# A layer of gated delta attention: the convolution taps of each head go round their three chains inside VectorE's places for that head

## The reference

```
outs = [dwconv_causal(x, w) for w in (ms_w3, ms_w15, ms_w31)]
y = jnp.concatenate(outs, axis=1)
y = y.reshape(b, h, 3 * d, l).transpose(0, 3, 1, 2)
y = y @ kernel_mix_w
```

## Time and profile before

| | us |
|---|---|
| median of 3 runs | 3498.72 |
| lowest and highest of them | 3491.64, 3504.08 |
| the profiled execution | 3488.17 |
| its span, from the first to the last instruction | 3485.9 |
| TensorE matmul busy (share of the span) | 3314.3 (95%) |
| VectorE busy | 3162.7 (91%) |
| ScalarE busy | 2760.5 (79%) |
| GpSimd busy | 824.9 (24%) |
| VectorE's taps (L1924), 5408 instructions | 2256.8 |

### The profile page before, as it was taken

The page is one execution under the profiler, slowest core; times in us unless marked ns, Lnnn a source line. Parts: engine busy times, 40 slices in busy tenths (PEclk is TensorE's granted clock), DMA queues, the critical chain, the costliest instruction groups (busy, mean ns, idle before and its releaser), DMA issues.

```text
span 3485.9 us, 70437 instructions
## 1 busy us (share of the span) xinstructions
PE 3314.3 (95%) x22880; PEld 2429.7 (70%) x22880; DVE 3162.7 (91%) x7841; ACT 2760.5 (79%) x9146; POOL 824.9 (24%) x1501
## 2 busy tenths in 40 slices
PE   7999999999999999999999999999999999999988
PEld 6666777667776677776777766777766777766764
DVE  6998999999898999999998999999999999999994
ACT  5777888778887778887788877788877788777874
POOL 2322221122221222211222212222112222112220
PEclk9999999999999999999999999999999999999999
DMA  6022211122211222111222112221112221112211
GB/s 188 18 40 51 51 33 39 31 51 51 49 30 26 50 51 51 37 37 29 51 51 50 29 31 45 51 51 40 34 29 51 51 51 32 39 32 51 45 30 21
DMA packets 188310, 154.96 MB, mean 44 GB/s; under 512 B 111804, under 2 KB 146108, under 8 KB 187688
## 3 DMA queue, kind: packets, MB, share of 16 engines
q0 software_dynamic: 31744, 79.70, 13.2%
q1 hardware_dynamic: 156200, 70.76, 7.7%
HBM read 51.34 MB, written 52.95 MB: 30 GB/s over the span
## 4 chain that ended last, share of the span: by engine, by line
DVE 30%; PE 27%; ACT 20%; issue 10%; DMA 9%; POOL 3%; SPq 0%; ACTq 0%; DVEq 0%; POOLq 0%
DVE my L1924 24%; PE dense L811 7%; DMA my<-prod 5%; PE dense L744 3%; PE dense L734 3%; ACT my L1361 3%; PE small L757 2%; ACT dense L1394 2%; PE cell L703 2%; PE dense L721 2%; DMA rows_out<-Bm 2%; PE cell L704 2%; POOL Tu L461 1%; POOL Xu L464 1%; DMA Bu<-rows_out 1%
## 5 line engine op out<-in xcount | busy, mean ns | idle before, releaser
L1924 DVE SCALAR_TENSOR_TENSOR my<-vT,mw,my 128x256 f32<-128x256 f32 x5408 | 2256.8, 483 | 44.8 <-DMA my<-prod 26.1
L422 POOL TENSOR_SCALAR vare<-xsq 128x2 f32<-128x2 f32 x32 | 6.0, 187 | 2008.3 <-ACT xsh L1104 2008.3
L811 PE MATMUL dense<-xsh,w 128*128 128x256 f32 x2016 | 474.5, 381 | 3.8
L811 PEld LDWEIGHTS dense<-xsh,w 128*128 128x128 f32 x2016 | 362.6, 190 | 70.9 <-ACT xr L1426 10.9
L1334 ACT ACTIVATE ka<-dense 128x512 f32<-128x512 f32 x64 | 38.2, 596 | 304.2 <-PE dense L721 304.2
L721 PE MATMUL dense<-xk,wfk 128*128 128x256 f32 x1024 | 239.7, 388 | 11.9 <-DVE xb L1992 11.7
L734 PE MATMUL dense<-wr,xr 128*128 128x512 f32 x512 | 241.2, 605 | 0.0
L744 PE MATMUL dense<-wfv,ka 128*128 128x512 f32 x512 | 238.2, 598 | 0.0
L574 PE MATMUL front<-xsh,wq 128*128 128x256 f32 x1024 | 236.5, 384 | 0.3 <-ACT raw L1142 0.3
L574 PE MATMUL front<-xsh,wv 128*128 128x256 f32 x1024 | 232.9, 386 | 2.7 <-ACT xsh L1119 2.7
L721 PEld LDWEIGHTS dense<-xk,wfk 128*128 128x128 f32 x1024 | 192.0, 192 | 62.0 <-issue 37.0
(11 more groups left out here) (188 smaller groups left out, 6806.3 us busy)
## 6 DMA issues: line engine op xcount, KB each, us to landing
my<-prod POOLq DMA_DIRECT2D x160, 384.0 KB, 4.2
xa<-in_x SPq DMA_DIRECT2D x32, 512.0 KB, 4.4
rows_out<-Bm SPq DMA_DIRECT2D x64, 256.0 KB, 4.2
out<-xb POOLq DMA_DIRECT2D x32, 512.0 KB, 14.7
Yq<-units_out SPq DMA_DIRECT2D x128, 32.0 KB, 2.3
w<-in_w SPq DMA_DIRECT2D x1, 2048.0 KB, 17.2
Bu<-rows_out SPq DMA_DIRECT2D x32, 64.0 KB, 3.0
units_out<-Xu SPq DMA_DIRECT2D x32, 64.0 KB, 2.5
```

What stands on the lines that cost most here:

```text
L811: e.matmul(by_batch(o), w1[:, k, hs(2 * pair + c)], xsh[s % 2][:, k, :, 1:1 + P], start=(k == 0), stop=False)
L1924: i = e.scalar_tensor_tensor(o, vT[s % 2][:, c, :, off:off + P], mw[:, col:col + 1], o, ALU.mult, ALU.add)
```

## The change

Only the order of calls in `vector_program` changes, and within it only the order of the taps of each head among the places which the taps of that head have. All other calls keep their place, counted in instructions, and no engine gets another instruction. In the loop, the new order goes round the three chains of a head. In head 2, where block 2 has 29 taps for VectorE and the others 13, block 2 has every second place and the other two share the rest. In the prologue and the epilogue, calls with adjoining ranges are written as one; the order there is the old one.

The head of the loop (head 3), the end of the loop's head 1 and the start of its head 2; what is left out follows the same patterns:

```
             for i in range(2, NS):
                 step_Y(i - 2)
-                taps(i - 2, 3, 9, 10)
+                taps(i - 2, 3, 5, 6)
                 taps(i - 2, 2, 34, 35)
                 taps(i - 2, 2, 53, 54)
-                taps(i - 2, 3, 5, 6)
-                taps(i - 2, 3, 8, 9)
+                taps(i - 2, 3, 8, 10)
                 turn_Y(i - 2, 1)
                 taps(i - 2, 3, 11, 12)
+                taps(i - 2, 3, 13, 14)
                 taps(i - 2, 3, 12, 13)
                 taps(i - 2, 3, 14, 15)
-                taps(i - 2, 3, 13, 14)
+                taps(i - 2, 3, 16, 17)
+                taps(i - 2, 3, 15, 16)
                 taps(i - 2, 3, 17, 18)
...
                 taps(i - 2, 3, 53, 54)
+                taps(i - 2, 3, 55, 56)
                 taps(i - 2, 3, 54, 55)
-                taps(i - 2, 3, 49, 50)
-                taps(i - 2, 3, 52, 53)
+                gate_value(i - 2, 0)
                 taps(i - 2, 3, 56, 57)
-                gate_value(i - 2, 0)
+                taps(i - 2, 3, 58, 59)
...
                 add_state(i - 2, 1)
-                taps(i - 1, 1, 13, 14)
-                taps(i - 1, 1, 15, 16)
-                taps(i - 1, 1, 10, 11)
-                taps(i - 1, 1, 17, 18)
+                taps(i - 1, 1, 11, 15)
                 norms_add(i - 1)
                 norms_inv(i - 1)
...
                 gains(i - 1)
-                taps(i - 1, 1, 20, 21)
-                taps(i - 1, 1, 22, 23)
-                taps(i - 1, 1, 25, 26)
-                taps(i - 1, 1, 24, 25)
-                taps(i - 1, 1, 27, 28)
+                taps(i - 1, 1, 23, 26)
+                taps(i - 1, 1, 0, 1)
+                taps(i - 1, 1, 26, 27)
                 softmax_sum(i - 2)
...
                 make_aT(i - 1, 0)
                 make_aT(i - 1, 1)
+                taps(i - 1, 2, 2, 3)
+                taps(i - 1, 2, 0, 1)
+                taps(i - 1, 2, 5, 6)
+                taps(i - 1, 2, 3, 4)
+                taps(i - 1, 2, 8, 9)
                 taps(i - 1, 2, 1, 2)
-                taps(i - 1, 2, 0, 1)
+                taps(i - 1, 2, 11, 12)
+                taps(i - 1, 2, 6, 7)
+                taps(i - 1, 2, 14, 15)
                 taps(i - 1, 2, 4, 5)
-                taps(i - 1, 2, 3, 4)
+                taps(i - 1, 2, 17, 18)
+                taps(i - 1, 2, 9, 10)
+                taps(i - 1, 2, 20, 21)
                 taps(i - 1, 2, 7, 8)
-                taps(i - 1, 2, 2, 3)
-                taps(i - 1, 2, 10, 11)
-                taps(i - 1, 2, 5, 6)
-                taps(i - 1, 2, 8, 9)
-                taps(i - 1, 2, 6, 7)
-                taps(i - 1, 2, 9, 10)
-                taps(i - 1, 2, 11, 12)
-                taps(i - 1, 2, 14, 15)
-                taps(i - 1, 2, 17, 18)
+                taps(i - 1, 2, 23, 24)
                 taps(i - 1, 2, 12, 13)
```

More of the change, by code:

```diff
@@ L2007, in vector_program @@
             taps(0, 0, 2, 3)
[L2008 to L2014, removed]
+            taps(0, 1, 1, 3)
+            taps(0, 1, 4, 7)
+            taps(0, 0, 3, 5)
             taps(0, 1, 7, 8)
@@ L2049, in vector_program @@
             gains(0)
-            taps(0, 1, 23, 24)
-            taps(0, 1, 24, 25)
-            taps(0, 1, 25, 26)
+            taps(0, 1, 23, 26)
             taps(0, 1, 3, 4)
@@ L2055, in vector_program @@
             taps(0, 1, 26, 27)
-            taps(0, 1, 28, 29)
-            taps(0, 1, 29, 30)
+            taps(0, 1, 28, 30)
             taps(0, 2, 5, 6)
@@ L2111, in vector_program @@
             taps(0, 2, 36, 37)
-            taps(0, 2, 49, 50)
-            taps(0, 2, 50, 51)
+            taps(0, 2, 49, 51)
             taps(0, 2, 28, 29)
@@ L2120, in vector_program @@
             taps(0, 3, 1, 2)
-            taps(0, 3, 3, 4)
-            taps(0, 3, 4, 5)
+            taps(0, 3, 3, 5)
             taps(0, 3, 7, 8)
@@ L2153, in vector_program @@
                 taps(i - 2, 3, 35, 36)
-                taps(i - 2, 3, 24, 25)
+                taps(i - 2, 3, 37, 38)
+                taps(i - 2, 3, 36, 37)
                 taps(i - 2, 3, 38, 39)
-                taps(i - 2, 3, 27, 28)
-                taps(i - 2, 3, 25, 26)
+                taps(i - 2, 3, 40, 41)
+                subtract_state(i - 2, 1)
+                taps(i - 2, 3, 39, 40)
                 taps(i - 2, 3, 41, 42)
-                taps(i - 2, 3, 30, 31)
-                taps(i - 2, 3, 28, 29)
@@ L2161, in vector_program @@
-                taps(i - 2, 3, 33, 34)
+                taps(i - 2, 2, 54, 55)
+                taps(i - 2, 3, 43, 44)
+                taps(i - 2, 3, 42, 43)
                 taps(i - 2, 3, 44, 45)
-                taps(i - 2, 3, 36, 37)
-                taps(i - 2, 3, 31, 32)
+                subtract_state(i - 2, 0)
+                taps(i - 2, 3, 46, 47)
+                taps(i - 2, 3, 45, 46)
                 taps(i - 2, 3, 47, 48)
-                subtract_state(i - 2, 1)
+                taps(i - 2, 3, 49, 50)
@@ L2167, in vector_program @@
+                taps(i - 2, 3, 48, 49)
                 taps(i - 2, 3, 50, 51)
[L2168 to L2178, removed]
+                taps(i - 2, 3, 52, 53)
@@ L2420, in vector_program @@
             taps(NS - 2, 3, 59, 60)
-            taps(NS - 2, 3, 61, 62)
-            taps(NS - 2, 3, 62, 63)
+            taps(NS - 2, 3, 61, 63)
             taps(NS - 2, 3, 64, 65)
@@ L2497, in vector_program @@
             taps(NS - 1, 1, 3, 4)
-            taps(NS - 1, 1, 28, 29)
-            taps(NS - 1, 1, 29, 30)
+            taps(NS - 1, 1, 28, 30)
             add_two(NS - 2, 0)
@@ L2553, in vector_program @@
             taps(NS - 1, 2, 28, 29)
-            taps(NS - 1, 2, 44, 45)
-            taps(NS - 1, 2, 45, 46)
+            taps(NS - 1, 2, 44, 46)
             make_aT(NS - 1, 0)
@@ L2565, in vector_program @@
             taps(NS - 1, 3, 3, 4)
-            taps(NS - 1, 3, 5, 6)
-            taps(NS - 1, 3, 6, 7)
+            taps(NS - 1, 3, 5, 7)
             taps(NS - 1, 2, 33, 34)
```

208 lines of the change are left out of this document (84 added, 124 removed).

## The result

The changed kernel takes 3586.07 us in the median (3574.16 to 3593.45, 4 runs), the kernel before 3497.98 beside it: 1.0249 of it as the ratio of the runs, 95% interval 1.0214 to 1.0283. By that ratio it is 87 us slower, far outside the range of 3470 to 3507. The profiled execution took 3589.27 us with a span of 3587.0, 101.1 longer than the span before.

What follows compares the result with a forecast made beforehand. No engine had room by itself (TensorE 95%, VectorE 91% busy), so waits decided, with head 3's fourth add limiting the long stretch. Gains of 3.9 + 3 + 2 = 9 us gave 3489.7 us from 3498.7; range 3470 to 3507.

Steps and rivals of the forecast that it cites:

- Price of a seam: VectorE's taps: one directly behind its own chain's tap costs 0.13 us; 12 an iteration, 47 us less VectorE work.
- Part 1: Head 3's seam between step_Y and subtract_state(0): VectorE is last there, so all counts, 3.9 us; bounds 0 and 3.9.
- Part 2: Seams ahead of feature_rest, norms_add and head 2's first tap: hidden by VectorE's waits there, together nothing.
- Part 3: Eight seams from head 2 to head 3's first tap: limited by head 3's fourth add, 0.1 us an iteration, 3 us.
- Part 4: GpSimd's inversion, advancing one instruction per VectorE instruction: fourth add 0.07 us sooner, 2 us, bounds +8 and -12.
- the lock between VectorE and GpSimd: VectorE instructions with two SBUF inputs and GpSimd ones reading SBUF exclude each other; said to change no figure.
- The slower rival: GpSimd's add into out, issued before the fourth add lands, delays it: 12 us loss, 3510.7; chance 0.1.

Runs made afterwards that it cites:

- e15: Kernel before with head 3's taps alone in their new order; 3482.69 us against 3492.59 beside it, ratio 0.9978.
- e17: Kernel before with head 1's taps alone in their new order, heads 2 and 3 old; ratio 1.0007 to the kernel before.
- e9: Changed kernel with one seam only, in head 2, about 4.5 us behind the landing of head 2's add; ratio 1.0035 to the kernel before.
- e11: Changed kernel with TensorE's turn_o(0) moved behind the two calls of project(4), filling its idle time; ratio 1.0274 to the kernel before.
- e10: Changed kernel with one seam only, in head 2, about 1.3 us behind the landing of head 2's add; ratio 1.0263 to the kernel before.
- e5: Changed kernel with one seam only, in head 2, about 3.3 us behind the landing of head 2's add; ratio 1.0046 to the kernel before.
- e7: Changed kernel with one small VectorE instruction, waiting for nothing, added behind head 2's sixteenth tap; ratio 1.0137 to the kernel before.
- e13: Kernel before with ScalarE's products for head 3's fourth add made ahead of copy_oT(1); ratio 1.0063 to the kernel before.

## Why the prediction was wrong

- **Price of a seam: right.** 17 taps shrank from 7.33 to 6.82 us. VectorE's busy time fell by 31.9 us and not 47, because a seam's 0.13 us is part overlap lost (0.08) and part a gap, and the gap never counted as busy.
- **Part 1 (head 3's seam, 3.9 us): right**, and hidden by the rest. The wait ahead of `solve` is 12.9 us where 17.3 - 3.9 = 13.4 was predicted. Alone (e15) the order gains 4.5 to 10.5 us.
- **Part 2 (three seams, nothing): right.** The covering waits grew from 70.1 to 72.3 and from 29.8 to 33.5 us, and e17 is level.
- **Part 3 (3 us, limited by the fourth add): the limit was right, the gain is not seen.** VectorE's wait for adds is 29.9 us in the changed kernel instead of the 50 expected, because VectorE is late as well there: ahead of `add_attention` it waits 76.0 us for `attend`, in the kernel before 9.4. Where GpSimd is on time (e9) the waits become 59 in number and 38.6 us, TensorE's wait for `xb` falls from 11.7 to 0.6 us and its wait for `mask_W`'s result rises from 19.7 to 27.6, as the part described, but no time is won.
- **Part 4 (GpSimd, "I take 0.07 us sooner at the fourth add: 2 us, bounds +8 and -12"): this step failed**, in sign and far beyond its bound. The fourth add lands 2.75 us later, 31 x 2.75 = 85 us. The rule behind it, "advances one instruction per instruction of VectorE", holds where GpSimd got in behind a break: the earlier trace rows show that stretch alone. I carried it over to the first instruction and priced a missed slot at 0.4 us, one tap. In a stream of taps without a break the slot doesn't come back until an instruction of another kind: L456 was released between 4.5 and 6.2 us and ended at 7.67, and L461 behind it lost its turn once more.
- The sentence that the lock between VectorE and GpSimd "changes none of the figures above" was the same mistake. The trace of before had the sign: L456 took 425 ns in the mean and 0.29 us where it had no wait, and its ends lay behind seams. I asked what the seams cost VectorE and not whom they let in.
- **The slower rival** had the right chain (a late fourth add) and the wrong cause. In e9 the add into `out` is issued ahead of the fourth add's landing in 17 of 29 iterations (4 in the kernel before), as the rival said, and the fourth add lands no later: at 28.80 us instead of 28.87.

## What to carry to other kernels

A pause on one engine can be another engine's only way in. Before a bubble is squeezed out, look at which instructions of other engines end just behind it, and ask where they would go instead. An engine that is 24% busy can hold the path: here GpSimd runs nearly without a pause from the inversion to the last add, and 2.31 us at its start cost 87 us in the changed kernel, some 4 us for each 0.1.

When a wait grows, fill it before blaming it: in e11 the wait shrank by 42.4 us and the time stayed, because the delay had a second road.

## What the runs showed of the hardware

- Beside VectorE's `scalar_tensor_tensor` with two tensors in SBUF (128x256, started every 0.396 us, each 0.08 us ahead of the end of the one before), a GpSimd `tensor_scalar` of 64x15 that takes 0.29 us alone took up to 3.2 us in the changed kernel and 3.6 in e10. Behind a break of the stream it got in at each of the next five boundaries in e5 and e9; the first refusal stood at the sixth in e9 and at the eighth in e5.
- Where it got in behind a break, the instructions behind it nearly always followed turn by turn, one boundary each, through taps without a break (e5: 0.24 us for the first of them). Where it got in behind `add_two` (changed kernel), the next one was refused again and took 1.45 us.
- A VectorE instruction of 128x1 with one tensor let it in without a break in the stream (e7, 30 of 30 iterations).
- Two DMAs issued 0.12 to 0.15 us apart, `units_out` and the fourth add, both took longer to land than where 0.38 us or more lay between them (e13: 3.44 us instead of 2.51, and 4.3 instead of 3.4 to 3.5).
